# Attention on pairs of heads, with both halves of the partitions in use, in a transformer layer with a mixture of experts

## The chip, the cores and the metric

The kernel runs on the 8 NeuronCores of one Trainium2 chip. Each core computes one sequence of the batch of 8, with the same program and its own `xt`; no core talks to another. The metric is the device time in microseconds of the slowest core, lower is better.

Engines: PE is TensorE (matmul), PEld its weight loads, DVE VectorE, ACT ScalarE, POOL GpSimd, SP SyncE.

## What is computed

Two blocks in sequence on x of shape 2048 x 1024 per core, each with a layernorm ahead and a residual behind. The change is in the first.

```python
x = x + attn(layernorm(x))            # 16 heads of 64 columns, one 64x192 Wqkv shared by all
x = x + ffn(layernorm(x))             # router over 8 experts, top 2, and a shared expert

# attn, for each head:
q, k, v = split(xh @ Wqkv + bqkv)     # xh: 2048 x 64
att = q @ k.T / sqrt(64)
mask = tril(ones(c, c), k=-1)
att = softmax(att * mask)             # masked entries are 0 ahead of the softmax, so they weigh exp(0) = 1
out = att @ v
# all heads side by side, then @ Wr + br
```

Because a masked entry counts as exp(0) = 1, key tiles above the diagonal aren't skipped in the product with v: there the left operand is a block of ones.

## The kernel before

Everything is held transposed, columns of the model on partitions: `XRES` (the residual, f32) and `XLN` (the layernorm's output, bf16) are 8 chunks of 128 partitions x 2048 tokens. Chunk `ch` of `XLN` holds head 2*ch in partitions 0 to 63 and head 2*ch+1 in partitions 64 to 127.

The program is written out by hand. `Plan.emit` (L48) puts an instruction at the end of its engine's queue, with its semaphore waits. An engine works in the order of emission, so the order of the text is the order of each engine. Waits on the DMA counters SQ and GQ are always taken on the count issued so far (L49): whoever waits for one of these DMAs waits for all that were issued on that counter before it.

Stages: layernorm 1, a barrier, loads of constants (`MASKS`, `IDB`, `WRF`, `BQKVC`, `BQKVR`, `BRR`), attention head by head, the projection with Wr (L499), a barrier, then layernorm 2, router and the experts.

Attention, for each of 16 heads:

1. Q and K (L336): for each of four blocks of 512 tokens one matmul for q and one for k, K = 64 rows, M = 64 columns, into partitions 0 to 63 of `PS4`; ACT adds the bias and writes `QT` or `KT` (L344), both 64 partitions. From the third block on a matmul waits for the eviction two blocks earlier of its own kind.
2. V (L353, L362): 16 token blocks, each a matmul with the weights and a one-row matmul with the bias, into `PS2`; one DVE copy of 128x1024 takes it to `VA` (L369), 16 groups of 65 columns of which the last is ones. The scores that follow on PE don't wait for this copy; the products with v do.
3. For each query block j = 0 to 3 (512 queries): 4j+4 score tiles of 128 keys x 512 queries (L393). They rotate over six PSUM slots. A score matmul waits for its slot and for the second last entry of `sc_hist`, a list in which the evictions of the tiles below the diagonal stand.
   - The first 4j tiles lie below the diagonal: ACT takes the exponential from PSUM into `PT` (L403), and this is entered in `sc_hist`.
   - The last four cross the diagonal: DVE multiplies by the mask into `SMASK` (L412), ACT takes the exponential from there (L417). The mask product waits for the exponential before it (`ss_exp_last`). These are not entered in `sc_hist`.
4. The product with v (L432): 4 query sub-blocks (`mt`) x 16 key tiles, 64 matmuls of 128x65 into `PS1`, the 65th column being the sum of the weights. The first waits for the last exponential.
5. The tail, four times (one per `mt`): DVE reciprocal of the sum from `PS1` (L444), DVE multiply from `PS1` into `AVN` (L449), PE transpose into `PTR` (L456), DVE copy into `AVT` (L468).

The next j, or the next head, starts on PE behind the fourth transpose. With 4 values of j and 16 heads there are 64 such blocks.

The mask operands are in f32: `c_masks` is 128 x 2048 f32, 1 MB.

Of the kernel before, what the change touches and what calls it, by code (L numbers as in the profile page):

```python
# [7 lines left out]
F32 = mybir.dt.float32  # L8
BF16 = mybir.dt.bfloat16
# [25 lines left out]
def _ckpt(ph):  # L35
    if DBG["stop"] == ph:
        raise _PhaseDone()
# [31 lines left out]
def build_program():  # L69
# [5 lines left out]
    bqkv_col = dt("bqkv_col", [64, 2], F32, kind="ExternalInput").ap()  # L75
# [12 lines left out]
    c_masks = dt("c_masks", [128, 4 * 512], F32, kind="ExternalInput").ap()  # L88
# [4 lines left out]
    with ExitStack() as ctx:  # L93
# [159 lines left out]
        try:  # L253
# [6 lines left out]
            with ExitStack() as actx:  # L260
                AE = actx.enter_context
                QT = AE(nc.sbuf_tensor("QT", [64, T], BF16))
                KT = AE(nc.sbuf_tensor("KT", [64, T], BF16))
                VA = AE(nc.sbuf_tensor("VA", [128, 16 * 65], BF16))
                PT = AE(nc.sbuf_tensor("PT", [128, 16 * 512], BF16))
                AVT = AE(nc.sbuf_tensor("AVT", [128, NCH * T], BF16))
                WRF = AE(nc.sbuf_tensor("WRF", [128, NCH * D], BF16))
                MASKS = AE(nc.sbuf_tensor("MASKS", [128, 4 * 512], F32))
# [4 lines left out]
                BQKVC = AE(nc.sbuf_tensor("BQKVC", [64, 2], F32))  # L273
# [41 lines left out]
                for h in range(min(H, DBG["nheads"])):  # L315
                    ch, off = h // 2, (h % 2) * 64
                    xh = XLN[off:off + 64, ch * T:(ch + 1) * T]

                    ev_q, ev_k = [], []
                    for s in (range(NTT) if DBG["qkv_parts"] in ("all", "qk") else []):  # L320
                        tsl = slice(s * 512, (s + 1) * 512)
                        for which in ("q", "k"):
                            base = 0 if which == "q" else 1024
                            slot_id = (0 if which == "q" else 2) + s % 2
                            psv = PS4[0:64, base + (s % 2) * 512: base + (s % 2) * 512 + 512]
                            wcol = 0 if which == "q" else 64
                            evs = ev_q if which == "q" else ev_k
                            if s >= 2:
                                w = [("SS", evs[s - 2])]
                            else:  # L330
                                w = [slot_free[slot_id]]
                            if s == 0 and which == "q":
                                w += [("SV", ln1_done), ("GQ", gq_wq)]
                            tq = P.emit("tensor",
                                        lambda e, psv=psv, wcol=wcol, tsl=tsl, xh=xh,
                                        off=off: e.matmul(  # L336
                                            psv, WQ[off:off + 64, wcol:wcol + 64],
                                            xh[:, tsl],
                                            start=True, stop=True),
                                        waits=w, inc="ST")  # L340
                            dst = (QT if which == "q" else KT)[0:64, tsl]
                            bias = BQKVC[0:64, 0:1] if which == "q" else BQKVC[0:64, 1:2]
                            evs.append(P.emit("scalar",
                                        lambda e, dst=dst, psv=psv, bias=bias: e.activation(  # L344
                                            dst, psv, AF.Identity, bias=bias),
                                        waits=[("ST", tq), ("GQ", gq_bqc)], inc="SS"))
                    tv_last = 0
                    for mt in (range(NMT) if DBG["qkv_parts"] in ("all", "v") else []):
                        psl = PS2[:, mt * 64:(mt + 1) * 64]
                        w = ([ps2_free, slot_free[4], slot_free[5],  # L350
                              ("SV", ln1_done)] if mt == 0 else [])
                        P.emit("tensor",
                               lambda e, psl=psl, mt=mt, ch=ch, off=off: e.matmul(  # L353
                                   psl,
                                   XLN[off:off + 64,
                                       ch * T + mt * 128: ch * T + (mt + 1) * 128],
                                   WQ[off:off + 64, 128:192],
                                   start=(mt in (0, 8)), stop=False,
                                   skip_group_check=True),
                               waits=w)  # L360
                        tv_last = P.emit("tensor",
                               lambda e, psl=psl: e.matmul(  # L362
                                   psl, ONES[0:1, 0:128], BQKVR[0:1, 128:192],
                                   start=False, stop=True, skip_group_check=True),
                               waits=([("GQ", gq_bqr), ("SQ", sq_ones)] if mt == 0 else []),
                               inc=("ST" if mt == NMT - 1 else None)) or tv_last
                    if DBG["qkv_parts"] in ("all", "v"):
                        sv_va = P.emit("vector",
                                   lambda e: e.tensor_copy(  # L369
                                       VA.ap().rearrange("p (g n) -> p g n", n=65)[:, :, 0:64],  # L370
                                       PS2.ap().rearrange("p (g n) -> p g n", n=64)),
                                   waits=[("ST", tv_last), ("SV", sv_vones)], inc="SV")
                    else:
                        sv_va = sv_vones
                    ps2_free = ("SV", max(sv_va, avt_done))
                    if h == 0:
                        _DBGREF["QT"], _DBGREF["KT"], _DBGREF["VA"] = QT, KT, VA
                        _ckpt("qkv")

                    rot = 0  # L380
                    for j in range(NTT):
                        for kc in range(4 * j + 4):
                            slot = rot % 6
                            rot += 1
                            psv = (PS4[:, slot * 512:(slot + 1) * 512] if slot < 4
                                   else PS2[:, (slot - 4) * 512:(slot - 3) * 512])
# [3 lines left out]
                            if kc == 0 and j == 0:  # L390
                                w += [("SS", ev_q[-1]), ("SS", ev_k[-1])]
                            ts = P.emit("tensor",
                                        lambda e, psv=psv, kc=kc, j=j: e.matmul(  # L393
                                            psv,
                                            KT[0:64, kc * 128:(kc + 1) * 128],
                                            QT[0:64, j * 512:(j + 1) * 512],
                                            start=True, stop=True),
                                        waits=w, inc="ST")
                            pts = PT[:, kc * 512:(kc + 1) * 512]
                            ptguard = [("ST", st_av_prev)] if kc == 0 else []  # L400
                            if kc < 4 * j:
                                ss_exp_last = P.emit("scalar",
                                        lambda e, pts=pts, psv=psv: e.activation(  # L403
                                            pts, psv, AF.Exp, scale=0.125),
                                        waits=[("ST", ts)] + ptguard, inc="SS")
                                slot_free[slot] = ("SS", ss_exp_last)
                                sc_hist.append(("SS", ss_exp_last))
                            else:
                                d = kc - 4 * j
                                smsl = SMASK[:, (kc % 2) * 512:(kc % 2) * 512 + 512]  # L410
                                vm = P.emit("vector",
                                        lambda e, smsl=smsl, psv=psv, d=d: e.tensor_mul(  # L412
                                            smsl, psv, MASKS[:, d * 512:(d + 1) * 512]),
                                        waits=[("ST", ts), ("SQ", sq_masks),
                                               ("SS", ss_exp_last)], inc="SV")
                                ss_exp_last = P.emit("scalar",
                                        lambda e, pts=pts, smsl=smsl: e.activation(  # L417
                                            pts, smsl, AF.Exp, scale=0.125),
                                        waits=[("SV", vm)] + ptguard, inc="SS")
                                slot_free[slot] = ("SV", vm)  # L420
# [692 lines left out]
```

How the kernel before makes its waits and increments, by code:

```python
        def run(e, _w=waits, _f=fn, _i=inc, _n=inc_n):  # L57
            for s, v in _w:
                e.wait_ge(sems[s], v)
            inst = _f(e)
            if _i is not None:
                inst.then_inc(sems[_i], _n)
```

## Time and profile before

| what | value |
|---|---|
| runs of before, us | 3943.6, 4241.51, 4313.21 (median 4241.51) |
| profiled execution, us | 3943.02 |
| its span on the slowest core (core 6) | 3941.5 |
| spans of the eight cores | 3936.2 to 3941.5 |
| busy share of the span | PE 74%, PEld 34%, DVE 30%, ACT 22%, POOL 1% |
| MASKS, WRF in the list of DMA issues | 1024.0 KB, 2048.0 KB (WRF as written; read as f32) |

The profiled execution's time is its span and 1.5 us around it, and it lies with the lowest of the three runs.

How to read it: the profile cuts the span into 40 slices of 98.5 us and gives the busy tenths of each engine, and the clock that was granted to TensorE, 10 being 2.4 GHz and 5 being 1.2 GHz. In a timeline each line is one or more merged instructions of one kind: start, duration, engine, line, operation, tiles, count, and in brackets how long the engine had sat idle before and what released it. A matmul's duration holds its latency; neighbouring matmuls overlap.

### The profile page before, as it was taken

The page shows a single profiled execution, that of the slowest core. Times are in us where ns is not written, and L with a number is a line of the kernel's source. Part 1 is how long each engine was busy: PE and PEld are TensorE (multiplying, and loading weights), DVE is VectorE, ACT ScalarE, POOL GpSimd, SP SyncE. Part 2 cuts the span into 40 slices and gives each one's busy share as a digit, 9 for nine tenths or more (in the row PEclk, how much of TensorE's full clock was granted, in tenths as well). Part 3 has the DMA queues.
Part 4 walks back from the last instruction along what each step waited for, and adds up shares of the span by engine and source line. Part 5 has one row for each costly group of instructions (what it writes and reads, how often), then busy time and mean ns, then how long its engine had stood idle before and what let it go on. Part 6 is the DMA issues. An engine that isn't in the chain of part 4 may idle for free.

```text
span 3941.5 us, 45987 instructions; the slowest of 8 cores (3936.2 to 3941.5 us)
## 1 busy us (share of the span) xinstructions
PE 2931.2 (74%) x15380; PEld 1344.2 (34%) x15380; DVE 1179.5 (30%) x2386; ACT 855.8 (22%) x1354; POOL 28.8 (1%) x55
## 2 busy tenths in 40 slices
PE   2355545455554545664999999999999999999997
PEld 0122222222222222221444444444444444444443
DVE  5222222222222222253133333333333332333332
ACT  0123332223222222100212221121222112122210
POOL 0000000000000000000000000000000000000000
PEclk7555555555555555686999999999999999999998
DMA  2100000000000000050022130402213040221302
GB/s 87 33 1 1 1 1 1 1 1 1 1 1 1 1 1 1 1 86 1 1 43 43 33 54 1 86 1 43 43 28 59 1 86 1 44 43 27 60 1 86
DMA packets 7087, 98.81 MB, mean 25 GB/s; under 512 B 1860, under 2 KB 2260, under 8 KB 2260
## 3 DMA queue, kind: packets, MB, share of 16 engines
q0 software_dynamic: 3984, 77.81, 11.6%
q1 hardware_dynamic: 2884, 18.06, 1.4%
q8 instruction: 140, 2.29, 0.2%
q14 instruction: 79, 0.65, 0.1%
HBM read 165.10 MB, written 8.39 MB: 44 GB/s over the span
## 4 chain that ended last, share of the span: by engine, by line
PE 70%; DVE 13%; issue 8%; ACT 7%; DMA 1%; DVEq 1%; ACTq 0%; SPq 0%; POOL 0%
PE PM L737 26%; PE PM L826 25%; PE PS L432 6%; DVE SMASK L412 5%; ACT PT L417 4%; PE PS L393 4%; ACT PT L403 3%; DVE AVN L449 2%; PE PTR L456 2%; PE PS L336 2%; PE PS L499 2%; DVE RZ L444 1%; PE PS L362 1%; PE PS L353 1%; DVE XLN L248 1%
## 5 line engine op out<-in xcount | busy, mean ns | idle before, releaser
L737 PE MATMUL PM<-XLN,W 128*128 128x512 bf16 x4608 | 1020.2, 385 | 0.7 <-DVE WSB L695 0.7
L826 PE MATMUL PM<-H1G,W 128*128 128x512 bf16 x4608 | 999.0, 379 | 0.0
L754 ACT ACTIVATE H1G<-PM,B1C 128x512 bf16<-128x512 f32 x576 | 395.9, 687 | 1611.3 <-PE PM L737 1611.3
L737 PEld LDWEIGHTS PM<-XLN,W 128*128 128x128 bf16 x4608 | 455.5, 99 | 561.9 <-issue 33.2
L826 PEld LDWEIGHTS PM<-H1G,W 128*128 128x128 bf16 x4608 | 450.8, 98 | 543.8
L432 PE MATMUL PS<-VA,PT 128*128 128x65 bf16 x2560 | 175.9, 242 | 349.8 <-ACT PT L417 349.8
L803 DVE TENSOR_TENSOR H1G<-H1G,WB 128x512 bf16<-128x512 bf16 x512 | 217.7, 425 | 686.1 <-ACT H1G L754 686.1
L841 DVE TENSOR_TENSOR XRES<-XRES,PM 128x512 f32<-128x512 f32 x288 | 198.0, 688 | 648.8 <-PE PM L826 648.8
L393 PE MATMUL PS<-QT,KT 64*128 64x512 bf16 x640 | 322.2, 600 | 73.1 <-ACT PT L403 72.6
L403 ACT ACTIVATE PT<-PS 128x512 bf16<-128x512 f32 x384 | 209.0, 595 | 564.9 <-PE PS L393 564.4
L412 DVE TENSOR_TENSOR SMASK<-PS,MASKS 128x512 f32<-128x512 f32 x256 | 176.9, 691 | 458.3 <-PE PS L393 285.5
L456 PE MATMUL PTR<-IDB,AVN 128*64 128x128 bf16 x256 | 68.6, 268 | 321.0 <-DVE AVN L449 321.0
L432 PEld LDWEIGHTS PS<-VA,PT 128*128 128x128 bf16 x2560 | 152.1, 131 | 406.0 <-issue 406.0
L417 ACT ACTIVATE PT<-SMASK 128x512 bf16<-128x512 f32 x256 | 161.1, 629 | 325.5 <-DVE SMASK L412 325.5
L847 DVE SCALAR_TENSOR_TENSOR XRES<-WB,B2C,XRES 128x512 f32<-128x512 bf16 x256 | 192.5, 752 | 47.1 <-DVE XRES L841 47.1
L393 PEld LDWEIGHTS PS<-QT,KT 64*128 64x128 bf16 x640 | 67.0, 107 | 278.4 <-issue 256.1
L456 PEld LDWEIGHTS PTR<-IDB,AVN 128*64 128x64 bf16 x256 | 31.2, 122 | 356.2 <-issue 356.2
L444 DVE RECIPROCAL RZ<-PS 128x1 f32<-128x1 f32 x256 | 41.3, 161 | 311.0 <-PE PS L432 307.8
L432 PE MATMUL PS<-VA,ONES 128*128 128x65 bf16 x1536 | 118.3, 242 | 0.0
L468 DVE COPY AVT<-PTR 64x128 bf16<-64x128 bf16 x256 | 56.8, 222 | 190.1 <-PE PTR L456 190.1
L336 PE MATMUL PS<-XLN,WQ 64*64 64x512 bf16 x128 | 62.7, 615 | 63.2 <-DMA BRR<-br_row 62.2
L432 PEld LDWEIGHTS PS<-VA,ONES 128*128 128x128 bf16 x1536 | 97.6, 131 | 0.0
(97 smaller groups left out, 835.3 us busy)
## 6 DMA issues: line engine op xcount, KB each, us to landing
W<-w1cat POOLq DMA_DIRECT2D x9, 4096.0 KB, 28.7
W<-w2cat POOLq DMA_DIRECT2D x9, 4096.0 KB, 27.8
XRES<-xt SPq DMA_DIRECT2D x8, 1024.0 KB
ot<-XRES SPq DMA_DIRECT2D x8, 1024.0 KB
WRF<-wr_rl POOLq DMA_DIRECT2D x1, 2048.0 KB, 19.1
MASKS<-c_masks SPq DMA_DIRECT2D x1, 1024.0 KB
B1C<-b1col POOLq DMA_DIRECT2D x9, 8.0 KB, 28.0
B2C<-b2col_t POOLq DMA_DIRECT2D x9, 4.0 KB, 3.4
```

The lines of the kernel that those rows point to most:

```text
L393: lambda e, psv=psv, kc=kc, j=j: e.matmul(psv, KT[0:64, kc * 128:(kc + 1) * 128], QT[0:64, j * 512:(j + 1) * 512], start=True, stop=True),
L403: lambda e, pts=pts, psv=psv: e.activation(pts, psv, AF.Exp, scale=0.125),
L412: lambda e, smsl=smsl, psv=psv, d=d: e.tensor_mul(smsl, psv, MASKS[:, d * 512:(d + 1) * 512]),
L417: lambda e, pts=pts, smsl=smsl: e.activation(pts, smsl, AF.Exp, scale=0.125),
L432: lambda e, lhs=lhs, mt=mt, kc=kc: e.matmul(PS1[:, mt * 65:(mt + 1) * 65], lhs, VA[:, kc * 65:(kc + 1) * 65], start=(mt == 0 and kc == 0), ...
L456: lambda e, mt=mt, off=off: e.transpose(PTR[off:off + 64, (mt % 2) * 128:(mt % 2) * 128 + 128], AVN[:, mt * 64:(mt + 1) * 64], IDB[:], til ...
L737: lambda e, psv=psv, kc=kc, ht=ht, tt=tt: e.matmul(psv, W1[:, kc * DFF + ht * 128: kc * DFF + (ht + 1) * 128], xln(kc)[:, tt * 512:(tt + 1 ...
L754: lambda e, h1sl=h1sl, psv=psv, e_i=e_i, ht=ht: e.activation(h1sl, psv, AF.Gelu, bias=B1C[:, (e_i % 2) * 16 + ht: (e_i % 2) * 16 + ht + 1]),
L803: lambda e, h1sl=h1sl, tt=tt: e.tensor_mul(h1sl, h1sl, WB[:, tt * 512:(tt + 1) * 512]),
L826: lambda e, psv=psv, kc=kc, dtl=dtl, buf=buf: e.matmul(psv, W2[:, kc * D + dtl * 128: kc * D + (dtl + 1) * 128], H1G[:, buf * 8192 + kc * 512:
L841: lambda e, psv=psv, dtl=dtl, tt=tt: e.tensor_add(xres(dtl)[:, tt * 512:(tt + 1) * 512], xres(dtl)[:, tt * 512:(tt + 1) * 512], psv),
L847: e.scalar_tensor_tensor(xres(dtl)[:, tt * 512:(tt + 1) * 512], wsrc, b2ap, xres(dtl)[:, tt * 512:(tt + 1) * 512], ALU.mult, ALU.add),
```

## The change

- Heads are worked in pairs (`hp`, `ch = hp`). `QT` and `KT` grow to 128 partitions, the even head in 0 to 63 and the odd one in 64 to 127; `VA` grows to two halves, `PT` becomes `PTE` and `PTO`, `BQKVC` gets 128 partitions.
- Q and K: for each block of 512 tokens and each of q and k one slot with two 64x64 matmuls, one into partitions 0 to 63 and one into 64 to 127, and two ACT evictions. The slots come from the same rotation of six as the scores and go by `slot_free` and `sc_hist[-2]`; `rot` runs on over the pairs instead of starting at 0 for each head.
- V: once for each head of the pair, both through `PS2`, so that the second waits for the copy of the first to `VA`; the pair's first score matmul waits for the second copy.
- Scores: even and odd head take turns tile by tile. Tiles on the diagonal are now also entered in `sc_hist`.
- The product with v: 64 matmuls for the even head, its tail, 64 for the odd head, its tail. Between product and tail DVE copies `PS1` (260 columns, f32) to a new SBUF tile `PAVS`, from which reciprocal and multiply read.
- Masks are bf16 in DRAM and in SBUF (0.5 MB).

The diff, cut to its core (what stood there before is described above, with its lines):

```diff
-    c_masks = dt("c_masks", [128, 4 * 512], F32, kind="ExternalInput").ap()
+    c_masks = dt("c_masks", [128, 4 * 512], BF16, kind="ExternalInput").ap()
...
-                QT = AE(nc.sbuf_tensor("QT", [64, T], BF16))
+                QT = AE(nc.sbuf_tensor("QT", [128, T], BF16))
...
+                PTE = AE(nc.sbuf_tensor("PTE", [128, 16 * 512], BF16))
+                PTO = AE(nc.sbuf_tensor("PTO", [128, 16 * 512], BF16))
+                PAVS = AE(nc.sbuf_tensor("PAVS", [128, 272], F32))
...
+                for hp in range((min(H, DBG["nheads"]) + 1) // 2):
+                    ch = hp
+                    ev_last = 0
+                    for sidx in range(NTT):
+                        tsl = slice(sidx * 512, (sidx + 1) * 512)
+                        for which, wcol in (("q", 0), ("k", 64)):
                             slot = rot % 6
                             rot += 1
+                            psv = slotap(slot)
                             w = [slot_free[slot]]
                             if len(sc_hist) >= 2:
                                 w.append(sc_hist[-2])
...
+                            for o in (0, 64):
+                                tq = P.emit("tensor",
+                                        lambda e, psv=psv, wcol=wcol, tsl=tsl, o=o,
+                                        ch=ch: e.matmul(
+                                            psv[o:o + 64, :],
+                                            WQ[o:o + 64, wcol:wcol + 64],
+                                            XLN[o:o + 64, ch * T:(ch + 1) * T][:, tsl],
+                                            start=True, stop=True,
+                                            skip_group_check=True),
+                                        waits=(w if o == 0 else []),
+                                        inc=("ST" if o == 64 else None)) or tq
...
+                            for o in (0, 64):
+                                ev_last = P.emit("scalar",
+                                        lambda e, dstt=dstt, psv=psv, o=o, tsl=tsl,
+                                        bcol=bcol: e.activation(
+                                            dstt[o:o + 64, tsl], psv[o:o + 64, :],
...
+                            slot_free[slot] = ("SS", ev_last)
+                            sc_hist.append(("SS", ev_last))
+                    sv_va = {}
+                    for oh in (0, 1):
...
+                            if mt == 0:
+                                w = [ps2_free, slot_free[4], slot_free[5]]
...
+                        ps2_free = ("SV", sv_va[oh])
+                    for j in range(NTT):
+                        for kc in range(4 * j + 4):
+                            for oh in (0, 1):
...
+                                if kc == 0 and j == 0 and oh == 0:
+                                    w += [("SS", ev_last), ("SV", sv_va[1])]
...
-                                            KT[0:64, kc * 128:(kc + 1) * 128],
-                                            QT[0:64, j * 512:(j + 1) * 512],
+                                            KT[o:o + 64, kc * 128:(kc + 1) * 128],
+                                            QT[o:o + 64, j * 512:(j + 1) * 512],
...
+                                    vm = P.emit("vector",
...
+                                            waits=[("ST", ts), ("SQ", sq_masks),
+                                                   ("SS", ss_exp_last)], inc="SV")
...
+                                    slot_free[slot] = ("SV", vm)
+                                    sc_hist.append(("SV", vm))
+                        for oh in (0, 1):
...
+                                    if mt == 0 and kc == 0:
+                                        w = [("SS", ss_exp_last), ps1_free]
...
+                            pcp = P.emit("vector",
+                                    lambda e: e.tensor_copy(PAVS[:, 0:260], PS1[:, 0:260]),
+                                    waits=[("ST", st_av), ("SV", ps1_free[1])], inc="SV")
+                            ps1_free = ("SV", pcp)
```

## Rows read from the trace of the kernel before

**Rows 1.** The page's 40 slices, TensorE's granted clock in tenths of full speed.

```profile
PEclk7555555555555555686999999999999999999998
```

**Rows 2.** The page's chain that ended last: share of the span by line.

```profile
PE PM L737 26%; PE PM L826 25%; PE PS L432 6%; DVE SMASK L412 5%; ACT PT L417 4%; PE PS L393 4%; ACT PT L403 3%; DVE AVN L449 2%; PE PTR L456 2%; PE PS L336 2%; PE PS L499 2%; DVE RZ L444 1%; PE PS L362 1%; PE PS L353 1%; DVE XLN L248 1%
```

**Rows 3.** Timeline of PE: attention's first matmul, and the projection's first behind it.

```profile
132.24 2.31 PE L336 MATMUL PS<-XLN,WQ 64*64 64x512 bf16 x5 [62.17 <-DMA BRR<-br_row]
...
1643.39 3.57 PE L499 MATMUL PS<-AVT,WRF 128*128 128x512 bf16 x8 [0.69 <-DVE AVT L468]
```

**Rows 4.** Timeline of head 4, block j = 1, from its first score matmul to the next block's.

```profile
534.37 1.02 PE L393 MATMUL PS<-QT,KT 64*128 64x512 bf16 x2
...
535.11 1.08 ACT L403 ACTIVATE PT<-PS 128x512 bf16<-128x512 f32 x2 [10.58 <-PE PS L393]
535.85 1.07 PE L393 MATMUL PS<-QT,KT 64*128 64x512 bf16 x2 [0.47 <-ACT PT L403]
...
537.27 1.86 PE L393 MATMUL PS<-QT,KT 64*128 64x512 bf16 x4 [0.35 <-ACT PT L403]
538.09 0.69 DVE L412 TENSOR_TENSOR SMASK<-PS,MASKS 128x512 f32<-128x512 f32 x1 [3.35 <-PE PS L393]
...
539.61 0.69 DVE L412 TENSOR_TENSOR SMASK<-PS,MASKS 128x512 f32<-128x512 f32 x1 [0.82 <-ACT PT L417]
...
544.45 0.60 PE L432 MATMUL PS<-VA,PT 128*128 128x65 bf16 x8 [5.32 <-ACT PT L417]
...
548.24 0.17 DVE L444 RECIPROCAL RZ<-PS 128x1 f32<-128x1 f32 x1 [4.90 <-PE PS L432]
...
549.23 0.28 PE L456 MATMUL PTR<-IDB,AVN 128*64 128x128 bf16 x1 [1.10 <-DVE AVN L449]
...
554.05 1.01 PE L393 MATMUL PS<-QT,KT 64*128 64x512 bf16 x2
```

**Rows 5.** Timeline of head 4 from its first matmul to block j = 0's product.

```profile
508.07 3.90 PE L336 MATMUL PS<-XLN,WQ 64*64 64x512 bf16 x8
...
508.83 0.68 ACT L344 ACTIVATE QT<-PS,BQKVC 64x512 bf16<-64x512 f32 x1 [10.71 <-PE PS L336]
...
509.41 0.67 ACT L344 ACTIVATE KT<-PS,BQKVC 64x512 bf16<-64x512 f32 x1
...
511.91 0.23 PE L353 MATMUL PS<-WQ,XLN 64*128 64x64 bf16 x1
...
517.13 1.88 PE L393 MATMUL PS<-QT,KT 64*128 64x512 bf16 x4
517.37 1.23 DVE L369 CAST VA<-PS 128x1024 bf16<-128x1024 f32 x1 [9.02 <-PE PS L362]
518.52 0.68 DVE L412 TENSOR_TENSOR SMASK<-PS,MASKS 128x512 f32<-128x512 f32 x1
...
524.91 0.38 PE L432 MATMUL PS<-VA,PT 128*128 128x65 bf16 x4 [5.89 <-ACT PT L417]
```

**Rows 6.** Groups of instructions by line: busy us, mean ns | idle before, releaser.

```profile
L803 DVE TENSOR_TENSOR H1G<-H1G,WB 128x512 bf16<-128x512 bf16 x512 | 217.7, 425 | 686.1 <-ACT H1G L754 686.1
...
L847 DVE SCALAR_TENSOR_TENSOR XRES<-WB,B2C,XRES 128x512 f32<-128x512 bf16 x256 | 192.5, 752 | 47.1 <-DVE XRES L841 47.1
...
L449 DVE TENSOR_SCALAR AVN<-PS,RZ 128x64 bf16<-128x64 f32 x256 | 72.6, 284 | 47.1 <-DVE RZ L444 46.6
...
L593 DVE COPY RLOG<-PR 8x512 f32<-8x512 f32 x4 | 2.7, 678 | 15.3 <-PE PR L589 15.3
L605 DVE COPY RT<-PTRK 128x8 f32<-128x8 f32 x16 | 2.7, 166 | 8.1 <-PE PTRK L598 8.1
...
L636 DVE COPY RCPR<-RCPR 128x64 f32<-128x64 f32 x1 | 0.2, 195 | 0.1
```

**Rows 7.** The page's DMA issues: KB, and us from issue to landing.

```profile
WRF<-wr_rl POOLq DMA_DIRECT2D x1, 2048.0 KB, 19.1
```

**Rows 8.** Timeline of PE, head 4, j = 2: the product's end at a higher clock.

```profile
569.54 0.55 PE L432 MATMUL PS<-VA,PT 128*128 128x65 bf16 x12
```

More of the change, by code:

```diff
@@ L313, in build_program @@
                 avt_done = 0
[L315 to L382, printed above, removed]
@@ new lines, in build_program, with slotap @@
+                st_av_prev = {0: 0, 1: 0}
+                rot = 0
+                def slotap(slot):
+                    return (PS4[:, slot * 512:(slot + 1) * 512] if slot < 4
+                            else PS2[:, (slot - 4) * 512:(slot - 3) * 512])
+                for hp in range((min(H, DBG["nheads"]) + 1) // 2):
[4 more added lines that the diff above has]
+                        for which, wcol in (("q", 0), ("k", 64)):
@@ L389, in build_program @@
                                 w.append(sc_hist[-2])
[L390 to L393, printed above, removed]
-                                            psv,
-                                            KT[0:64, kc * 128:(kc + 1) * 128],
-                                            QT[0:64, j * 512:(j + 1) * 512],
-                                            start=True, stop=True),
+                            if sidx == 0 and which == "q" and hp == 0:
+                                w += [("SV", ln1_done), ("GQ", gq_wq)]
@@ new lines, in build_program @@
+                    for j in range(NTT):
+                        for kc in range(4 * j + 4):
+                            for oh in (0, 1):
+                                o = oh * 64
+                                slot = rot % 6
+                                rot += 1
+                                psv = slotap(slot)
+                                w = [slot_free[slot]]
+                                if len(sc_hist) >= 2:
+                                    w.append(sc_hist[-2])
+                                if kc == 0 and j == 0 and oh == 0:
+                                    w += [("SS", ev_last), ("SV", sv_va[1])]
+                                ts = P.emit("tensor",
+                                        lambda e, psv=psv, kc=kc, j=j, o=o: e.matmul(
+                                            psv,
+                                            KT[o:o + 64, kc * 128:(kc + 1) * 128],
+                                            QT[o:o + 64, j * 512:(j + 1) * 512],
+                                            start=True, stop=True,
+                                            skip_group_check=True),
@@ L398, in build_program @@
                                         waits=w, inc="ST")
[L399 to L420, printed above, removed]
```

193 lines of the change are left out of this document (126 added, 67 removed).

## The prediction

> **What bounds the kernel now.** I read the page's slices first, for where the change can act. TensorE's granted clock [rows 1] splits the run: about two slices at the start, then attention up to slice 17 with nearly all slices at 5, which is 1.2 GHz, then router and experts at 9. Attention runs from 132.24 to 1643.39 [rows 3], so 1511 us or 94.4 a head; the other 2430 us are out of the change's reach. The chain that ended last [rows 2] says which engine sets attention: none. Its lines take turns: products with v 6%, mask 5%, the two exponentials 4% and 3%, scores 4%, tail 2+2+1%. It is one long dependency chain, so a step is worth its latency, and what an engine does less of is worth nothing. The timeline of one block [rows 4] gives the links:
>
> - Below the diagonal: matmuls start in pairs 1.42 us apart (535.85, 537.27). The loop is matmul, exponential, and the wait for the second last eviction: 0.71 a tile. From the first score to the first mask product (534.37 to 538.09) 3.72 = two such pairs and 0.88 of filling.
> - On the diagonal: mask products 1.52 apart (538.09, 539.61), each released by the exponential before it. Four tiles and the hand-over to PE: 538.09 to 544.45 = 6.36.
> - Product with v and tail: 544.45 to 554.05 = 9.60, of which the product is 3.79 (to the reciprocal).
>
> The head's front [rows 5]: Q, K and V take PE from 508.07 to 517.13 = 9.06, of it V 5.22. The copy to `VA` (517.37, 1.23 long) lies beside the first scores and holds only the first mask product up. Block j = 0 is 517.13 to 524.91 = 7.78 up to its product.
>
> **The change, part by part.** I price a pair of heads against two heads of before. Three things do not move. The tile rate below the diagonal stays 1.42 for two tiles, since the same wait holds. The mask product still waits for the exponential before it, so the 256 diagonal tiles stay at 1.52. PE's order is product, tail, product, tail, so the odd head's product stands behind the even head's fourth transpose; it is not laid into the tail. All 64 tails stay on the path, and freeing `PS1` earlier frees nothing that PE could start on.
>
> 1. *Blocks j = 1 to 3, shared filling.* Before, twice (3.72 + 6.36) = 20.16 for j = 1. After: 8 tiles below the diagonal = 4 x 1.42 = 5.68, filling 0.88 once, and 8 diagonal tiles = 6.36 + 4 x 1.52 = 12.44: 19.00. Gain 1.16, the same for j = 2 and 3. 24 blocks: **-27.8**.
> 2. *Block j = 0.* Before 2 x 7.78 = 15.56. After, with V copied already, the first mask product comes 0.82 after the first score (as 537.27 to 538.09 [rows 4]): 0.82 + 12.44 = 13.26. Gain 2.30, 8 pairs: **-18.4**.
> 3. *Q and K.* Before, the two heads' fronts are 18.12. After, each slot has two evictions, ACT starts one every 0.58 (508.83, 509.41 [rows 5]), and a slot's matmuls wait for the eviction two slots back. The eighth slot's matmuls follow the sixth slot's second eviction, the twelfth in all: 0.76 + 11 x 0.58 + 0.68 = 7.8, 0.1 to the matmul, and 0.4 for its stream: V starts at 8.3.
> 4. *V.* Twice 5.22 = 10.44. The copy is now open twice: 0.24 from PE's end to its start, 1.23, and about 0.3 back to PE (an estimate; tile hand-overs in rows 4 are 0.1 to 0.4) = 1.77, twice 3.54: once because the second V waits for `PS2`, once because the first score waits. Front: 8.3 + 10.4 + 3.5 = 22.3. Since `rot` runs on (88 slots a pair, 88 mod 6 = 4), pairs 1, 4 and 7 use slots 4 and 5, which lie in `PS2`, last, and V there waits for the final eviction: 10.3 instead of 8.3, on average 0.75. Parts 3 and 4 together 23.0 - 18.1 = 4.9 a pair, 8 pairs: **+39.2**.
> 5. *Copy `PS1` to `PAVS`.* Not in the trace. The nearest rows are copies out of PSUM with 8 elements in 0.166 and 512 in 0.678 [rows 6]; on their line 260 take 0.42. A DVE step waiting for the one before adds 0.18 (reciprocal at 548.24 to transpose at 549.23 is 0.99, less 0.17 and 0.28, over three hand-overs [rows 4, 6]). 0.60 x 64 = **+38.4**. Bounds: 0.17 + 0.1, +17; 0.68 + 0.18, +55. Nothing covers it, as PE's next instruction is the transpose that waits for it.
> 6. *Reciprocal and multiply from SBUF.* A copy of 64 from SBUF takes 0.195, one of 8 from PSUM 0.166: no sign of a cheaper SBUF. I take **0**; were the multiply as quick as that 0.195 instead of 0.284, 256 x 0.09 = -23.
> 7. *bf16 masks.* The product still has an f32 operand from PSUM. L847, which mixes bf16 and f32, takes 0.752 for 512; the all-bf16 one L803 takes 0.425 [rows 6]. The mixed row is the nearer: **0**. Were it 0.425, -0.27 x 256 = -68. The load: attention's first matmul waits 62 us, last for the constants' DMAs [rows 3]; WRF needs 19.1 to land [rows 7] beside 1 MB of masks, with its own 4 MB to read. Half a megabyte less of five: a tenth of 19.1, **-1.9**.
> 8. *Diagonal tiles in `sc_hist`.* A new wait: their matmul may start only when the mask product two back is done, where before it ran up to six slots ahead. From there to the mask product that needs it lie exponential, mask product, exponential: 1.52 x 2 - 0.69 = 2.35; matmul to mask needs 0.82. Covered, **0**; without the cover it is 256 x 0.82 = +210.
>
> Sum: -27.8 - 18.4 + 39.2 + 38.4 - 1.9 = +29.5, on 3943.0: **3972 us**, 0.7% more.
>
> On part 6 the Trainium skill ("VectorE: DVE Perf Modes", the section on the TRN2 errata) says otherwise: 58 fixed cycles for SBUF sources against 120 for PSUM, 65 ns less each. By it, as an estimate, two operations x 256 x 0.065 = -33, and the sum would be about 3939. The fixed part in rows 6 doesn't fall for SBUF, so the sum above goes by the rows.
>
> **The rivals.**
>
> - *Packing pays.* Even and odd scores lie in different halves of the partitions, Q and K in opposite quadrants. If the score stage ran at ACT's own pace, two exponentials in 1.08 [rows 4], it would save 0.34 x 192 pairs = -65: 3907. Against it: the matmul that follows waits for the second last eviction as before, and starts 0.46 after its neighbour because of that wait, not for lack of array. The Trainium skill ("TensorE: Matmul & The Clock Gate", Part 3) has such matmuls start 4 ns apart, with up to 3.07 times the speed for four; the trace of before has no such pair. Conversely, if the two Q (or K) matmuls run one after the other, each slot's loop grows from 2.28 to 2.56 for two slots, +1.4 a pair, +11: 3984.
> - *The clock rises.* Attention has 1.2 GHz almost throughout; near the end of a product 12 matmuls took 0.55 [rows 8], where at 1.2 GHz 8 take 0.60 [rows 4]. At 2.4 GHz all through, products would fall from 3.79 to about 2.3 (-95), score pairs by 0.2 (-38), V by a third (-28): 3810. The product, the only stage with such rows, keeps its length and its pause behind, so I see no reason for more of it.
> - *Slower: the wait of part 8 binds.* Place: each diagonal tile. It decides from the point at which matmul to mask takes over 2.35; then up to 0.82 a tile comes onto the path, +210: 4180. The 0.82 would have to nearly triple.
>
> **How the numbers follow.** Forecast 0.76; packing pays 0.08; clock 0.06; the new wait 0.04; the rest, 0.06, for something in the pair order that I don't see, either way. Around the forecast the unknown costs give: low 3972 - 21 (copy) - 23 (multiply) = 3928; high 3972 + 17 + 11, and 15 if the mask product takes L847's 0.752, = 4015. The change's own range against the profiled execution is 3905 to 4015, with packing in it. The recorded time is a median of runs, though, and those of before spread from 3943.6 to 4313.2 with the median 298 over the profiled execution, a spread that one profiled execution doesn't explain. The change adds to either level: the median would become 4271. The range must hold that too: 3905 to 4300. About 2% (79 us) is what a measurement of this kernel can tell from no change. Same: the forecast 0.76 less a little, and packing, 0.80. Faster: the clock and a share of the rest, 0.10. Slower: the new wait and a share of the rest, with the fronts worse than priced, 0.10.
>
> **What would show it.** The timeline of a pair: first Q matmul to first score 22 to 25; mask products still 1.52 apart; pairs below the diagonal still 1.42; a copy of about 0.42 in front of each reciprocal, 64 in all; multiply at 0.27 to 0.28; the chain from product to the next product or score 10.2 instead of 9.6; attention about 1540 long, ending near 1671. I am wrong if the score pairs go under 1.3, if the granted clock in attention is at 2.4 GHz for more than a small part, or if diagonal tiles are over 1.6 apart.

## The result, and the profile after

| | before | after |
|---|---|---|
| median of ten runs, us | 3943.38 | 3978.18 |
| lowest of them | 3942.27 | 3977.64 |
| profiled execution's span (slowest core) | 3941.5 (core 6) | 3976.8 (core 4) |

The ratio after to before is 1.0088, 95% interval 1.0078 to 1.0099: 0.9% slower, within 2%, but clear of no change. With both kernels one or two of the ten runs came out some 8% longer on the cores of one half of the chip; such runs are left out of every ratio here, stages are read from a core of the half that was not disturbed, and the other runs lie within 2.1 us of one another before and 1.1 after.

The page's granted clock after, against [rows 1]:

```profile
PEclk7555555555555555595999999999999999999998
```

Attention still runs at 1.2 GHz. Its first pair of heads, from the timeline of the changed kernel, against [rows 5]:

```profile
130.98 1.06 PE L342 MATMUL PS<-XLN,WQ 64*64 64x512 bf16 x4 [60.88 <-DMA BRR<-br_row]
131.76 1.39 ACT L355 ACTIVATE QT<-PS,BQKVC 64x512 bf16<-64x512 f32 x2 [66.26 <-PE PS L342]
133.18 1.39 ACT L355 ACTIVATE KT<-PS,BQKVC 64x512 bf16<-64x512 f32 x2
133.30 0.63 PE L342 MATMUL PS<-XLN,WQ 64*64 64x512 bf16 x2 [1.26 <-ACT QT L355]
134.59 1.39 ACT L355 ACTIVATE QT<-PS,BQKVC 64x512 bf16<-64x512 f32 x2
...
140.94 0.23 PE L374 MATMUL PS<-WQ,XLN 64*128 64x64 bf16 x1
...
146.41 1.23 DVE L390 CAST VA<-PS 128x1024 bf16<-128x1024 f32 x1 [34.61 <-PE PS L383]
148.00 0.21 PE L374 MATMUL PS<-WQ,XLN 64*128 64x64 bf16 x1 [1.76 <-DVE VA L390]
...
153.54 1.23 DVE L390 CAST VA<-PS 128x1024 bf16<-128x1024 f32 x1 [5.91 <-PE PS L383]
154.91 0.81 PE L409 MATMUL PS<-QT,KT 64*128 64x512 bf16 x2 [1.55 <-DVE VA L390]
```

Two matmuls in opposite quadrants last 0.63 together, no longer than one, and start 0.004 apart where in the kernel before the second starts 0.40 behind the first: the array does run them side by side. It gains nothing, for ACT's two evictions of a slot take 1.41 (131.76, 133.18, 134.59) and PE waits for them. V waits 1.76 for its first copy, the first score 1.55 for the second.

The odd head's tail of the first block and the first score matmuls of block j = 1, against [rows 4]:

```profile
181.60 0.43 DVE L473 COPY PAVS<-PS 128x260 f32<-128x260 f32 x1 [3.57 <-PE PS L460]
182.13 0.16 DVE L480 RECIPROCAL RZ<-PAVS 128x1 f32<-128x1 f32 x1
182.47 0.26 DVE L485 TENSOR_SCALAR AVN<-PAVS,RZ 128x64 bf16<-128x64 f32 x1 [0.17 <-DVE RZ L480]
183.09 0.22 PE L492 MATMUL PTR<-IDB,AVN 128*64 128x128 bf16 x1 [1.66 <-DVE AVN L485]
...
187.99 0.81 PE L409 MATMUL PS<-QT,KT 64*128 64x512 bf16 x2
...
189.48 1.07 PE L409 MATMUL PS<-QT,KT 64*128 64x512 bf16 x2 [0.67 <-ACT PTE L422]
190.90 1.07 PE L409 MATMUL PS<-QT,KT 64*128 64x512 bf16 x2 [0.35 <-ACT PTE L422]
```

The copy stands in front of the reciprocal, and the transpose waits 1.66 where it waited 1.10 [rows 4]. Score pairs start 1.42 apart, as before. The groups of the changed kernel by line, against [rows 6]:

```profile
L433 DVE TENSOR_TENSOR SMASK<-PS,MASKS 128x512 f32<-128x512 f32 x256 | 177.1, 692 | 480.4 <-PE PS L409 378.2 <-ACT PTO L422 58.8 <-ACT PTE L439 35.0
L485 DVE TENSOR_SCALAR AVN<-PAVS,RZ 128x64 bf16<-128x64 f32 x256 | 65.0, 254 | 46.7 <-DVE RZ L480 46.4
L473 DVE COPY PAVS<-PS 128x260 f32<-128x260 f32 x64 | 27.4, 428 | 264.8 <-PE PS L460 264.8
```

A mean mask product takes 692 ns with bf16 masks and 691 with f32. The multiply fell from 284 to 254. The first line puts most of DVE's idle time ahead of a mask product down to a score matmul (378.2 of 480.4 us), not to the exponential that the text of the kernel makes it wait for. In the timeline the two end at the same moment, 157.09, and the profile names one of them:

```profile
156.46 0.63 ACT L439 ACTIVATE PTE<-SMASK 128x512 bf16<-128x512 f32 x1 [13.39 <-DVE SMASK L433]
156.51 0.58 PE L409 MATMUL PS<-QT,KT 64*128 64x512 bf16 x1 [0.78 <-DVE SMASK L433]
157.19 0.69 DVE L433 TENSOR_TENSOR SMASK<-PS,MASKS 128x512 f32<-128x512 f32 x1 [0.82 <-PE PS L409]
```

Experiments 4 and 7 tell which of the two holds it.

I added up PE's timeline by stage, each from its first matmul to the next stage's first, over all of attention (64 products, 16 heads or 8 pairs), on the slowest core of each kernel. "Fronts" are the first two rows:

| stage, us | before | after | difference | predicted |
|---|---|---|---|---|
| Q and K, to the first V | 61.6 | 86.5 | +24.9 | with the next row |
| V, to the first score | 83.7 | 111.8 | +28.1 | fronts together +39.2 |
| scores, to the product | 744.8 | 696.6 | -48.2 | -46.2 |
| product, to the first transpose | 301.6 | 340.8 | +39.2 | +38.4 |
| transposes, to what follows | 319.4 | 313.1 | -6.3 | 0 |
| start of attention | 132.24 | 130.98 | -1.3 | -1.9 |

With -1.1 behind attention that is the +35.3 between the spans. Below, a stage's sum is told in this way, in experiments 1 to 8 on core 0, from 9 on on core 4. On core 0 the changed kernel's attention is 1546.9 (Q and K 86.4, V 112.0, scores 696.5, product 340.0, transposes 312.0), the kernel before's 1511.5.

### The profile page after: what moved, and what is told of

The parts are those of the page before. It is cut to its first block, busy times and chain, and to the rows that moved or that the text cites. A ratio compares the mean times of both kernels' runs of the same rounds, so it can differ in the third digit from the quotient of the medians.

```text
span 3976.8 us, 45742 instructions; the slowest of 8 cores (3974.0 to 3976.8 us)
## 1 busy us (share of the span) xinstructions
PE 2922.8 (73%) x15189; PEld 1336.5 (34%) x15380; DVE 1200.0 (30%) x2450; ACT 869.5 (22%) x1354; POOL 29.2 (1%) x55
## 4 chain that ended last, share of the span: by engine, by line
PE 67%; DVE 13%; ACT 9%; issue 8%; DMA 1%; DVEq 1%; ACTq 0%; SPq 0%; POOL 0%
PE PM L771 25%; PE PM L860 25%; PE PS L460 6%; DVE SMASK L433 5%; PE PS L409 3%; ACT PTE L422 3%; ACT PTO L439 2%; ACT PTE L439 2%; PE PTR L492 2%; DVE AVN L485 2%; PE PS L533 1%; DVE RZ L480 1%; PE PS L383 1%; PE PS L374 1%; DVE XLN L248 1%
## 5 line engine op out<-in xcount | busy, mean ns | idle before, releaser
L409 PE MATMUL PS<-QT,KT 64*128 64x512 bf16 x640 | 344.9, 582 | 258.6 <-DVE SMASK L433 171.5
L433 DVE TENSOR_TENSOR SMASK<-PS,MASKS 128x512 f32<-128x512 f32 x256 | 177.1, 692 | 480.4 <-PE PS L409 378.2
L422 ACT ACTIVATE PTE<-PS 128x512 bf16<-128x512 f32 x192 | 114.6, 597 | 565.2 <-PE PS L409 564.4
L460 PE MATMUL PS<-VA,PTE 128*128 128x65 bf16 x1280 | 88.6, 243 | 105.5 <-ACT PTO L439 105.5
L439 ACT ACTIVATE PTE<-SMASK 128x512 bf16<-128x512 f32 x128 | 80.5, 629 | 230.6 <-DVE SMASK L433 230.6
L460 PEld LDWEIGHTS PS<-VA,PTE 128*128 128x128 bf16 x1280 | 76.5, 131 | 120.8 <-issue 120.8
L422 ACT ACTIVATE PTO<-PS 128x512 bf16<-128x512 f32 x192 | 113.7, 592 | 3.2 <-PE PS L409 2.5
L342 PE MATMUL PS<-XLN,WQ 64*64 64x512 bf16 x128 | 38.9, 619 | 102.2 <-DMA BRR<-br_row 60.9
L473 DVE COPY PAVS<-PS 128x260 f32<-128x260 f32 x64 | 27.4, 428 | 264.8 <-PE PS L460 264.8
## 6 DMA issues: line engine op xcount, KB each, us to landing
WRF<-wr_rl POOLq DMA_DIRECT2D x1, 2048.0 KB, 17.3
```

The source lines that it names most:

```text
L409: lambda e, psv=psv, kc=kc, j=j, o=o: e.matmul(psv, KT[o:o + 64, kc * 128:(kc + 1) * 128], QT[o:o + 64, j * 512:(j + 1) * 512], start=True ...
L422: lambda e, pts=pts, psv=psv: e.activation(pts, psv, AF.Exp, scale=0.125),
L433: e.tensor_mul(smsl, psv, MASKS[:, d * 512:(d + 1) * 512]),
L439: lambda e, pts=pts, smsl=smsl: e.activation(pts, smsl, AF.Exp, scale=0.125),
L460: e.matmul(PS1[:, mt * 65:(mt + 1) * 65], lhs, VA[:, oh * 1040 + kc * 65: oh * 1040 + (kc + 1) * 65], start=(mt == 0 and kc == 0), stop=(k ...
```

## The experiments

**1. Without the copy to PAVS.**

```diff
-  pcp = tensor_copy(PAVS[:, 0:260], PS1[:, 0:260]);  ps1_free = ("SV", pcp)
-  reciprocal and multiply read PAVS
+  reciprocal and multiply read PS1;  ps1_free = the fourth multiply
```

> The changed kernel without the copy of PS1 to PAVS: reciprocal and multiply read PS1 as before, and PS1 is free again behind the fourth multiply. Theory A (the copy is on the path, 0.61 us in each of 64 tails = -39.2, and its SBUF source gives back 0.03 in each of 256 multiplies = 6.4 in all): 33 us less than the changed kernel, about 3945, ratio to before 1.0005. Rival B (the early release of PS1 is worth something): less than 20 us gained. In the trace: product to first transpose 4.7 instead of 5.3, multiply 0.284 instead of 0.254.

Measured: ratio to before 1.0023 (0.9974 to 1.0072); attention 1517.1, 29.8 less; product stage 340.0 to 302.9, transposes 312.0 to 317.9, multiply 284 again. The product stage fell by 0.58 for each of 64 tails, the copy's price. Reading from PSUM again costs 6 in the transposes, which is what the SBUF sources had given back. Without the early release of `PS1` nothing got longer by more than the scores' 1.5, so it had gained next to nothing.

**2. One eviction of 128 partitions for a slot.**

```diff
-  for o in (0, 64): activation(dstt[o:o+64, tsl], psv[o:o+64, :], Identity, bias=BQKVC[o:o+64, ...])
+  activation(dstt[:, tsl], psv[:, :], Identity, bias=BQKVC[:, ...])
```

> The changed kernel with one ACT eviction of 128 partitions for a Q or K slot instead of two of 64. Theory A (ACT's evictions, 16 of 0.71 a pair, set the front): a slot's loop becomes matmul 0.76, eviction 0.68, wait 0.12 = 1.56 for two slots, V starts about 5.5 us after the first Q matmul instead of 10.0, and in pairs 1, 4 and 7 about 6.6 instead of 12.2: 8 x 4.9 = -39 us, about 3939, ratio 0.999. Rival B (the front is set by PE or by something else): under 10 us gained.

Measured: ratio 1.0003 (0.9962 to 1.0044); attention 1512.4; Q and K 86.4 to 51.2, -35.2. The timeline of core 0:

```profile
129.88 0.69 ACT L354 ACTIVATE QT<-PS,BQKVC 128x512 bf16<-128x512 f32 x1 [65.49 <-PE PS L342]
130.47 0.68 ACT L354 ACTIVATE KT<-PS,BQKVC 128x512 bf16<-128x512 f32 x1
130.72 1.21 PE L342 MATMUL PS<-XLN,WQ 64*64 64x512 bf16 x4 [0.56 <-ACT QT L354]
131.50 0.69 ACT L354 ACTIVATE QT<-PS,BQKVC 128x512 bf16<-128x512 f32 x1 [0.35 <-PE PS L342]
```

An eviction of 128 partitions takes the same 0.68 as one of 64. The changed kernel had packed the matmuls and left the evictions, the bound, unpacked. This one edit takes it level with the kernel before, whose Q and K take 61.6: with matmuls and evictions both packed they gain 10, while V and its copies still take 28 more.

**3. The halves of a K slot evicted in the other order.**

```diff
+  oo = (0, 64) if which == "q" else (64, 0)
-  for o in (0, 64):
+  for o in oo:
```

> The changed kernel with the two evictions of a K slot in the other order (64 first, then 0), so that ACT changes its half of the partitions 8 times a pair instead of 16. Theory A (an eviction behind one in the other half can't overlap with it, 0.71 apart; in the same half 0.58): spacing alternates 0.71 and 0.58, V starts 0.7 us earlier in each pair (1.0 in three of them), -6 us, about 3972. Rival B (the 0.71 comes from something else, the two waits of a slot or the upper half itself): spacing stays 0.71, time stays 3978.

Measured: ratio 1.0053 (1.0025 to 1.0081), too wide to tell 6 us. The stage tells: Q and K 86.4 to 80.3, -6.1. Core 0's timeline:

```profile
130.50 1.39 ACT L356 ACTIVATE QT<-PS,BQKVC 64x512 bf16<-64x512 f32 x2 [65.78 <-PE PS L342]
131.80 1.38 ACT L356 ACTIVATE KT<-PS,BQKVC 64x512 bf16<-64x512 f32 x2
133.08 1.38 ACT L356 ACTIVATE QT<-PS,BQKVC 64x512 bf16<-64x512 f32 x2
```

Inside a slot the half changes, and the two last 1.38 as before (the second starts 0.70 behind the first). Across slots it no longer does, and a slot begins 1.28 to 1.30 after the last one instead of 1.41: 0.58 behind its predecessor, the spacing of [rows 5]. The change of half costs 0.13. A pair of the changed kernel has it 15 times, 11 of them ahead of the eviction that V's start hangs on, and all 15 in pairs 1, 4 and 7. The edit takes away 5 of the 11 and 7 of the 15, and V starts 0.67 and 0.94 earlier.

**4. Diagonal tiles out of the list.**

```diff
   slot_free[slot] = ("SV", vm)
-  sc_hist.append(("SV", vm))
```

> The changed kernel with the diagonal tiles left out of the list of evictions that score matmuls wait for, as before. Theory A (the added wait is covered): within 2 us of 3978. Rival B (the added wait costs): diagonal stage closer together, up to 210 us less. The trace of the changed kernel has some mask products released by the matmul and not by the exponential (0.82 behind it), and the four blocks' score stages came out within 0.1 of the sum, so I expect under 5 us.

Measured: ratio 1.0105 (0.9981 to 1.023); attention 1546.5, scores 696.6 against 696.5, mask products 1.52 apart as before. The interval is too wide for the ratio to say anything; by the stages the added wait is covered and costs nothing.

**5. Q and K in slots 0 to 3, the copy's wait moved.**

```diff
-  slot = rot % 6                       # Q and K
+  slot = rot % 4                       # rot = 0 at the start of the pair and of its scores
+  slot_free[4] = slot_free[5] = ("SV", sv_va[1])
-  w += [("SS", ev_last), ("SV", sv_va[1])]
+  w += [("SS", ev_last)]
```

> The changed kernel with Q and K in slots 0 to 3 alone, scores starting at slot 0, and the wait for the second V copy moved from the first score to the first use of slots 4 and 5. Theory A (the two waits priced in parts 3 and 4 are real): V of pairs 1, 4 and 7 no longer waits for the last eviction, 3 x 2.3 = -6.8; the first score starts 1.6 earlier but its mask product still stands behind the copy, 8 x 1.0 = -8: in all -15 in attention. Rival B (the copies lie beside other work anyway): under 4.

Measured: ratio 1.0019 (0.9987 to 1.005); attention 1529.9, -17.0: Q and K -6.6, V -13.3, scores +4.9, since the first mask product still stands behind the copy on DVE.

**6. Scores six deep.**

```diff
   w = [slot_free[slot]]
-  if len(sc_hist) >= 2: w.append(sc_hist[-2])
```

> The changed kernel with the wait of a score matmul for the second last eviction taken away, so that only its own slot (six) holds it. Theory A (below the diagonal that wait, not the array, keeps packing from paying): two tiles at ACT's pace, 1.09 instead of 1.42, 192 pairs, -60 in attention, the diagonal unchanged at 1.52. Rival B (the loop is matmul latency and would stay): under 10 gained.

Measured: ratio 0.9862 (0.9809 to 0.9914); attention 1462.7; scores 696.5 to 613.3, -83. Core 0's timeline:

```profile
186.14 5.50 PE L407 MATMUL PS<-QT,KT 64*128 64x512 bf16 x14
186.89 0.60 ACT L420 ACTIVATE PTE<-PS 128x512 bf16<-128x512 f32 x1 [21.06 <-PE PS L407]
187.39 0.59 ACT L420 ACTIVATE PTO<-PS 128x512 bf16<-128x512 f32 x1
187.86 0.60 ACT L420 ACTIVATE PTE<-PS 128x512 bf16<-128x512 f32 x1
188.34 0.62 ACT L420 ACTIVATE PTO<-PS 128x512 bf16<-128x512 f32 x1
```

Exponentials start 0.48 apart without a gap, 0.95 a pair instead of 1.42. I had expected 1.09, the duration of two merged ones, and 60 us; their starts can lie closer. Mask products stay 1.52 apart. The wait for the second last eviction had set the pace below the diagonal.

**7. The mask product two exponentials back.**

```diff
-  waits=[..., ("SS", ss_exp_last)]
+  waits=[..., ("SS", sm_free[smi])]    # the exponential that read this SMASK buffer
```

> The changed kernel with the mask product waiting for the exponential that last read its own SMASK buffer, two tiles back, instead of the last exponential. Theory A (diagonal tiles are held by that wait): 0.8 a tile instead of 1.52, 224 tiles behind the first of their block, -160 in attention. Rival B (DVE and ACT are bound there by their work): 0.69 + 0.63 a tile stay apart, under 30 gained.

Measured: ratio 0.97 (0.9595 to 0.9804); attention 1383.7; scores 537.1, -159.4. Core 0's timeline:

```profile
187.53 0.63 ACT L441 ACTIVATE PTE<-SMASK 128x512 bf16<-128x512 f32 x1 [1.26 <-DVE SMASK L435]
187.58 1.18 PE L411 MATMUL PS<-QT,KT 64*128 64x512 bf16 x2 [0.59 <-DVE SMASK L435]
188.13 0.63 ACT L441 ACTIVATE PTO<-SMASK 128x512 bf16<-128x512 f32 x1
188.41 1.29 DVE L435 TENSOR_TENSOR SMASK<-PS,MASKS 128x512 f32<-128x512 f32 x2 [0.38 <-PE PS L411]
189.19 0.63 ACT L441 ACTIVATE PTE<-SMASK 128x512 bf16<-128x512 f32 x1 [0.44 <-DVE SMASK L435]
```

Two tiles in 1.66 (187.53, 189.19) instead of 3.04, so it was the exponential that held the mask product. Here the mask products are released by the matmuls (0.38 <-PE): with this wait gone the next bound is the score matmul's wait for the second last entry of `sc_hist`. Experiment 11, with both waits gone, bears that out: its scores fall by 282, where 83 and 159 add up to 242.

**8. Both products ahead of the tails.**

```diff
   product(even); copy to PAVS[0]; 4 x (reciprocal, multiply) of even
+  product(odd);  copy to PAVS[1]
   4 x (transpose, copy) of even
-  product(odd);  copy to PAVS
   4 x (reciprocal, multiply, transpose, copy) of odd
```

`AVN`, `RZ` and `PAVS` hold both heads, and an even transpose waits for the last copy out of `PTR`.

> The changed kernel with both heads' products issued ahead of the tails; the copy to PAVS frees PS1, and the even head's four reciprocals and multiplies lie beside the odd head's product. Theory A (the copy is worth its 0.61 only if PE gets something to do behind it): a block's two products and tails take 18.2 instead of 20.4 us, -70 in attention, so faster than the kernel before. Rival B (the odd product only moves the even tail back): 0 or slower.

Measured: ratio 0.9725 (0.9672 to 0.9778); attention 1416.9, -130 instead of the -70 expected: the products' stage 340.0 to 234.1, transposes 312.0 to 287.8. Core 0's stretches, first an even product and the odd one behind it, then the same two of another block (columns: length, busy us of PE, PEld, DVE, ACT, POOL, granted clock, DMA share, GB/s):

```profile
380.20:383.80 3.60, 3.46 (x64) 3.35 (x64) 0.00 (x0) 0.00 (x0) 0.00 (x0) 0.58 0.02 5
384.40:386.50 2.10, 2.07 (x64) 2.10 (x64) 1.26 (x7) 0.00 (x0) 0.00 (x0) 1.00 0.00 0
466.40:470.00 3.60, 3.58 (x64) 3.53 (x64) 0.00 (x0) 0.00 (x0) 0.00 (x0) 0.50 0.00 0
470.80:474.40 3.60, 3.55 (x64) 3.54 (x64) 1.67 (x8) 0.00 (x0) 0.00 (x0) 0.50 0.02 5
```

Right behind the even product the odd one is granted 2.4 GHz in 15 of the 32 blocks, and its 64 matmuls then last 2.23 from start to end; in the other 17 it stays at 1.2 GHz and takes 3.7, as in the second pair of stretches. What decides between them isn't shown. The 15 are worth about 22 of the 130. The main gain doesn't need the clock: between the end of the even product and the odd one's start lie 0.75 instead of a whole tail, and the wait for copy, reciprocal and multiply is paid once a block instead of twice. The even tail's steps, two thirds of them at 0.68 to 0.76 instead of 1.4 to 1.6, add to it. This is what the copy to `PAVS` is good for, and the changed kernel didn't use it.

**9. All of it, on pairs.** Experiments 2, 5, 6, 7 and 8, and a shorter tail:

```diff
+  1 reciprocal for 4 columns, 4 multiplies (each head)
+  8 transposes into PTR[128, 512], one copy of 128x512 to AVT
```

> All that gained, on pairs of heads: one eviction of 128 partitions, Q and K in slots 0 to 3, scores six deep, mask product two back, both products ahead of the tails, and in the tail one reciprocal for four columns, four multiplies, eight transposes into one PTR of 512 columns and one copy of 128x512 for both heads. Summing what each gained alone in attention (-35, -17, -83, -159, -130) and some 5 us a block for the shorter tail (-150), about 1547 - 574 = 970 of attention, and 3400 in all. Rival (the gains overlap, since with the waits gone ACT or DVE is the bound): a third of it is lost, 3600.

Measured: ratio 0.8374 (0.8313 to 0.8436), median 3320.11, beating both kernels; attention 874.4 on core 4: Q and K 46.6, V 98.5, scores 413.3, products 219.6, transposes 96.4 (from 312.0). Its timeline:

```profile
290.71 0.43 DVE L491 COPY PAVS<-PS 128x260 f32<-128x260 f32 x1 [4.82 <-PE PS L478]
291.24 0.18 DVE L448 RECIPROCAL RZ<-PAVS 128x4 f32<-128x4 f32 x1
291.29 0.42 PE L478 MATMUL PS<-VA,PTO 128*128 128x65 bf16 x8 [0.75 <-DVE PAVS L491]
...
291.60 0.78 DVE L456 TENSOR_SCALAR AVN<-PAVS,RZ 128x64 bf16<-128x64 f32 x4 [0.18 <-DVE RZ L448]
...
293.44 0.90 PE L500 MATMUL PTR<-IDB,AVN 128*64 128x128 bf16 x4
...
295.19 1.23 PE L500 MATMUL PTR<-IDB,AVN 128*64 128x128 bf16 x4 [0.85 <-DVE AVN L456]
296.42 1.07 PE L408 MATMUL PS<-QT,KT 64*128 64x512 bf16 x6
```

From the odd product's first matmul to the next score 5.1 us, both tails in it; this is one of the 24 blocks of 32 whose odd product has 2.4 GHz, the others take about 1.5 longer. The gains did not overlap; the sum of 3400 was beaten by 80, and in attention's stages that is some 56 in products and tails and 46 in the scores. The latter are for the most part the 40 by which the two loosened waits together beat their sum (experiment 11).

**10 and 11. What pairing itself is worth**: the two loosened waits (experiments 6 and 7) on the kernel before and on the changed one.

> The kernel before, head by head, with the same two waits loosened: scores six deep, mask product two back. Against the next run it tells what pairing itself is worth. Theory A (pairing gives only the shared filling): score stages fall from 745 by about as much as in pairs (-83 and -159, -240 in all), so about 500, and attention ends 35 us shorter than in the paired kernel with both waits loosened. Rival B (with the waits gone the packed score matmuls pay): the paired kernel is at least level.

> The changed kernel with both waits loosened. Theory A: -240 in attention, about 1305, 3735 in all, and slower than the unpaired kernel with the same waits by about 35 (fronts +53, copies +39, less 7 from SBUF reads, less what the shared filling saves, 48). Rival B: score matmuls of the two halves overlap in the array, the score stage falls by more than in the unpaired one, and the paired kernel is level or faster.

Measured: unpaired 0.9311 (0.9223 to 0.9399), attention 1246.6; paired 0.935 (0.9282 to 0.9419), attention 1263.0 where 1305 was expected, on core 4. The ratios can't tell the two apart; the stages can: scores 478.1 and 414.4, a difference of 64 for the pairs where it was 48 with the tight waits; Q, K and V 145.2 and 198.2, products 305.0 and 339.3, transposes 318.3 and 311.1. The paired kernel is 16 longer, less than the 35 of theory A and not level as in B. Of the 64, pairs save 2.9 us in a block j = 0 and 1.1 in one of j = 3, most where there are fewest tiles below the diagonal, as shared filling would have it. Below the diagonal the exponentials of both kernels start 0.48 apart: both go at ACT's pace there, so overlap in the array can't shorten it. How much of the 64 is overlap at the start of a block wasn't taken apart.

**12. bf16 masks alone, on the kernel before.** The changed kernel has no room for f32 masks: with them 64 bytes a partition are left in SBUF where `BRR` needs 2048. So the narrower masks make room for the second `PT`.

> The kernel before with the masks in bf16 and nothing else (the other way round there is no room in SBUF). Theory A (the product has an f32 operand in PSUM and doesn't get faster; only the load is shorter): mask product stays at 0.691, attention starts 1 to 2 us earlier, time within 3 us of before. Rival B (bf16 masks speed the product up): 0.43 instead of 0.69, -68.

Measured: ratio 0.9987 (0.9948 to 1.0025); attention 1510.8 long, the same to 0.1 us as before's on core 4, mask product 691; attention starts at 128.0 on core 4 and 129.9 on core 0, before's profile has 132.4 and 131.7. The product gives nothing. On the load: on this chip and core 4 attention starts at 132.0 with f32 masks (experiment 10) and at 128.0, 129.4 and 130.0 with bf16 ones (12, 11, 9), 2 to 4 earlier; between the profiles of the changed kernel and of before it was 0.2 (core 0) to 1.3. With the same masks the start moves by 2 from run to run, so its size isn't settled closer than that.

## Why the prediction was right or wrong

The sum gave +29.5, the medians differ by +34.8; 3972 against 3978.18. That the two lie so near is in part luck: the fronts alone came out 13.8 over their term, and the transposes (-6.3 for 0), the scores (-2.0 more than said) and small terms took 8 of it back. Two steps failed: the spacing of evictions in part 3, and the last one, from a sum of +29.5 to "same". Point by point:

- *What bounds it* and *what does not move*: right. 1.42, 1.52 and the tails on the path all stood, and experiments 6, 7 and 8 showed what held each.
- *Parts 1 and 2, shared filling*: -46.2 predicted, -48.2 measured.
- *Part 3, Q and K*: the mechanism right, the size wrong, and the largest miss. The term that failed is "ACT starts one every 0.58". That spacing was read from evictions that all lay in partitions 0 to 63; in the changed kernel they alternate, 0.71 apart, and V starts 9.96 after the first matmul, not 8.3, and 12.2, not 10.3, in the three pairs with slots 4 and 5. The spacing, 11 or 15 times 0.13, is 13 of the 14 us over eight pairs; the rest is matmul and hand-over at the end, priced a little short. Fronts +53.0 instead of +39.2.
- *Part 4, V and its copies*: 13.98 a pair, as predicted to the hundredth (10.44 + 3.54). The single waits are 1.76 and 1.55 instead of 1.77 twice, and V with the first copy 7.06, so the hundredth is luck.
- *Part 5, the copy*: +38.4 predicted, +39.2 measured, 0.428 against 0.42 for the copy. Nothing covered it. About 2 of the 39.2 are not the copy's: a product takes 3.65 on the mean where it took 3.61, as the granted clock rises within fewer of them.
- *Part 6, SBUF sources*: I took 0 and the bound was -23; measured -6.3 in the transposes, and experiment 1 gives them back. The multiply is 0.030 shorter. The Trainium skill ("VectorE: DVE Perf Modes", errata section) would have had 0.065 on each of both operations. The multiply got half of it, the reciprocal 0.004 (161 to 157).
- *Part 7*: right on the mask product. `WRF` lands after 17.3 instead of 19.1, the tenth that was forecast; attention's start moved by 0.2 to 4 by core and run, around the 1.9 said.
- *Part 8, the new wait*: covered (experiment 4).
- *The rivals*: packing is physically there (0.63 for two) and pays nothing, for the reason given against it; the clock stayed at 1.2 GHz, and of that rival's prices only the product's is shown, 2.23 in experiment 8 for the 2.3 said, while no run shows those for scores and V; the new wait didn't bind.
- *What would show it*: of the signs, first Q matmul to first score is 23.9 in five pairs and 26.2 in the three with slots 4 and 5, outside 22 to 25; attention is 1548.8 long, not 1540; the multiply takes 0.254, under 0.27 to 0.28; the chain from product to the next product or score is 10.2, as said.
- *How the numbers follow*: this step failed too. I took 2% for what a measurement can tell, put 0.80 on "same" and 0.10 on "slower", and stretched the range to 4300 for the spread of three runs. Ten runs of each kernel had medians 34.8 apart with about 2 us of scatter, and the interval of the ratio, 1.0078 to 1.0099, lies clear of 1. The sum of my own terms, +29.5 with both large costs laid open on the path, said slower; I should have said that the sign was clear and its size small. The range of the change itself, 3905 to 4015, was enough.

## What to carry to other kernels

Packing two matmuls into the array was worth something here only once what empties PSUM was packed with them (86.4 for Q and K without, 51.2 with it, 61.6 unpacked); look first at which engine or wait sets the pace of the loop, and pack the evictions. The copy that frees a buffer early paid only when the next user of the buffer was issued ahead of the rest of the chain (experiment 8). Two waits tighter than the buffers need cost far more here (83 and 159 us, experiments 6 and 7) than the change could win.

## What the runs showed of the hardware

- ACT evictions out of PSUM start 0.58 us apart when they stay in one half of the partitions, and 0.71 when the half changes from one slot to the next (experiment 3). 128 partitions cost as much as 64 (0.68).
- Two 64x64 matmuls in opposite quadrants last 0.63 us together, one alone 0.60 to 0.63.
- A product of 64 matmuls with 0.75 us between it and the one before was granted 2.4 GHz in 15 of 32 blocks (24 of 32 in experiment 9) and lasted 2.23 us instead of 3.68; behind a tail or the wait for the last exponential, all 64 products of the changed kernel had a mean granted clock of 0.50 to 0.60 of full speed.
- A DVE multiply of 128x64 with a per-partition scalar takes 254 ns from SBUF and 284 from PSUM.
- A DVE product of 128x512 with one f32 operand in PSUM takes 691 ns, whether the other is f32 or bf16 in SBUF (experiment 12).
